# Graph-convolution kernel on one core: Euler pieces in the pauses of the tridiagonalization, and a re-ordered Newton step

## The reference, cut to what matters

```python
h = relu(layernorm(x)); x = x + L0(h)        # Euler stage
h = relu(layernorm(x)); x = x + L1(h)        # graph convolution in the eigenbasis
h = relu(layernorm(x)); x = x + L2(h)
h = relu(layernorm(x)); x = x + L3(h)
# L0: 8 steps on h = x @ fc_w.T + fc_b, with w_eff = w * clip(d, 0, 1) @ w.T
f = sigmoid(alpha)[:, None] * 0.5 * (adj @ h - h) + h @ w_eff - h + x0
h = h + f / 8
# L1: deg = row sums + column sums - diagonal of A
L_norm = deg**-0.5 * (diag(deg) - A) * deg**-0.5
_, U = eigh(L_norm)
out = U @ (relu((U.T @ h) @ W1 + b1) @ W2 + b2)
```

## Time and profile before

| | us |
|---|---|
| median of 3 runs | 4941.13 (4937.12 to 4941.86) |
| the profiled execution, its own time | 4943.4 |
| its span | 4941.6 |
| PE (matmul) busy | 3781.6 (77%) |
| DVE busy | 3279.5 (66%) |
| ACT busy | 1064.3 (22%) |
| POOL busy | 413.0 (8%) |

### The profile page before, as it was taken

The page is one execution under the profiler, slowest core; times in us unless marked ns, Lnnn a source line. Parts: engine busy times, 40 slices in busy tenths (PEclk is TensorE's granted clock), DMA queues, the critical chain, the costliest instruction groups (busy, mean ns, idle before and its releaser), DMA issues.

```text
span 4941.6 us, 71519 instructions
## 1 busy us (share of the span) xinstructions
PE 3781.6 (77%) x20546; PEld 1897.0 (38%) x20546; DVE 3279.5 (66%) x20976; ACT 1064.3 (22%) x4173; POOL 413.0 (8%) x1793
## 2 busy tenths in 40 slices
PE   4777777777778888888875667748965957599998
PEld 2333333333333333333354333425542623244433
DVE  5777777878888888888877898998822122202323
ACT  1111111222222222222201111101112122314542
POOL 0000000000000000000022221101100000000000
PEclk8999999999999999999956878879977978689998
DMA  2000000000000000000000000000000000000000
GB/s 86 2 1 1 2 1 1 2 1 1 2 1 1 1 2 1 1 1 1 1 1 1 1 1 1 1 0 1 1 0 0 0 17 0 0 0 0 0 0 34
DMA packets 3109, 21.11 MB, mean 4 GB/s; under 512 B 432, under 2 KB 560, under 8 KB 1072
## 3 DMA queue, kind: packets, MB, share of 16 engines
q1 hardware_dynamic: 2736, 16.85, 0.9%
HBM read 12.66 MB, written 4.19 MB: 3 GB/s over the span
## 4 chain that ended last, share of the span: by engine, by line
PE 48%; DVE 44%; ACT 3%; issue 3%; DMA 0%; POOL 0%; DVEq 0%; SPq 0%; POOLq 0%; ACTq 0%
PE ps L554 7%; PE ps L524 7%; PE ps L834 6%; DVE jq L1245 4%; PE ps L558 3%; PE ps L546 3%; DVE C L1424 2%; PE ps L841 2%; DVE tsc L1408 2%; DVE WG L1365 2%; DVE tsc L1418 2%; PE ps L530 2%; DVE tsc L1398 2%; DVE TMP L1360 2%; PE ps L806 1%
## 5 line engine op out<-in xcount | busy, mean ns | idle before, releaser
L546 PE MATMUL ps<-eye,same 128*128 128x512 f32 x2040 | 1200.4, 672 | 0.0
L563 PE MATMUL ps<-dots,ones 128*128 128x3 f32 x1020 | 199.2, 265 | 368.1 <-DVE dots L1245 367.5
L563 PEld LDWEIGHTS ps<-dots,ones 128*128 128x128 f32 x1020 | 161.4, 197 | 805.2 <-DVE dots L1245 803.8
L554 PEld LDWEIGHTS ps<-C 128*32 128x32 f32 x10200 | 255.2, 114 | 522.3 <-DVE C L1424 441.0
L554 PE MATMUL ps<-C 128*32 128x131 f32 (+39 forms) x10200 | 373.8, 277 | 76.1 <-DVE C L1424 21.3
L1079 ACT ACTIVATE sz<-C,tsc 128x4 f32<-128x4 f32 (+3 forms) x510 | 151.6, 297 | 1022.6 <-DVE tsc L1415 1022.6
L546 PEld LDWEIGHTS ps<-eye,same 128*128 128x128 f32 x2040 | 328.9, 203 | 0.0
L524 PE MATMUL ps<-C,LT 128*128 128x512 f32 x512 | 244.2, 622 | 91.9 <-ACT C L1071 91.9
L834 PE MATMUL ps<-C,V 128*128 128x512 f32 (+1 forms) x504 | 287.5, 727 | 8.5 <-issue 7.5
L884 POOL TENSOR_TENSOR xm<-C,WK 128x4 f32<-128x4 f32 (+3 forms) x510 | 101.0, 198 | 2275.0 <-DVE C L1424 1917.2
L1077 ACT ACTIVATE tsc<-tsc 128x1 f32<-128x1 f32 x510 | 103.4, 203 | 841.4 <-DVE tsc L1378 841.4
(11 more groups left out here) (468 smaller groups left out, 7127.4 us busy)
## 6 DMA issues: line engine op xcount, KB each, us to landing
out_x<-X SPq DMA_DIRECT2D x4, 1024.0 KB, 3.9
X<-in_x SPq DMA_DIRECT2D x2, 1280.0 KB, 20.5
X<-in_x SPq DMA_DIRECT2D x1, 1536.0 KB, 16.8
eye<-in_eye SPq DMA_DIRECT2D x1, 1026.0 KB, 9.4
WK<-in_adj SPq DMA_DIRECT2D x1, 1024.0 KB, 4.9
adjT<-in_adjT SPq DMA_DIRECT2D x1, 1024.0 KB, 7.0
WK<-in_below SPq DMA_DIRECT2D x1, 1024.0 KB, 11.2
V<-in_wih SPq DMA_DIRECT2D x1, 1024.0 KB, 4.9
```

What stands on the lines that cost most here:

```text
L546: mm(ps[:, 7, 0:n], ident, eye[:, 0, 0:n], start=True, stop=True)
L554: mm(ps[q * QUAD:(q + 1) * QUAD, 0, 0:c + n], SI[:, b, 0, 2 * j:2 * j + 1].broadcast_to([P, QUAD]), AS[:, b, q, k * QUAD:P + n], start=(b ...
L563: mm(ps[:, 3, 0:3], ones[:], dots[:], start=True, stop=True).then_inc(S["dots_ps"], 1)
```

## The change

1. The Euler work leaves the front and the tree. `plan_gaps` cuts it into pieces and puts each into one of the two pauses of a reflection (`pause`); a pause without a piece keeps its idle matmul. A piece whose data come from an eviction may only stand in a first pause after the reflection in which ScalarE evicts (`at`); the pieces of a unit follow each other pause by pause. ScalarE evicts at most one item per reflection, after `saved`; POOL adds to X after its unit vector.
2. `ln_root(0)` stands directly behind `table_fill` on ScalarE.
3. The idle matmul goes to bank 2; the panel's transposes to banks 2 and 3, since Euler uses 4 to 7.
4. In a Newton step the coefficients are formed in place in QF, with the factor -4 in c, one paired product, and the absolute value on ScalarE; X8 is formed before the clamp.
5. At the start of a level POOL scales LE by -4 gap and makes L8; VectorE does neither.
6. Below level 7 the two products for F2 are one instruction.

```diff
+REFLECTIONS = N - 2
...
+    def __init__(self):
+        self.tensor, self.scalar, self.pool = {}, {r: [] for r in range(REFLECTIONS + 2)}, {r: [] for r in range(REFLECTIONS + 2)}
+        self.gap, self.seen = 0, {}
+    def at(self, key, r):
+        while len(self.scalar[r]) > 0:
+            r += 1
+        self.scalar[r].append(key)
+        self.seen[key] = r
+        return r
+    def unit(self, key, parts):
+        for part, needs in enumerate(parts):
+            g = max([self.gap] + [2 * self.seen[n] for n in needs])
+            self.tensor[g] = key + (part,)
+            self.gap = g + 1
+        return self.at(key, g // 2 + 1 if g % 2 == 0 else g // 2 + 2)
+def plan_gaps():
+    p = Gaps()
+    p.at(("fill", 0), 0)
+    last = ("fill", 0)
+    for u in range(EULER):
+        p.unit(("table", u), [[last]] * ((u + 1) // 3 + 1))
+        last = ("table", u)
+    p.unit(("out", 0), [[last]] * 4)
+    last = ("out", 0)
+    for u in range(EULER + 1):
+        p.unit(("w", u), [[last]] * KB)
+        last = ("w", u)
+    first = 1
+    for t in range(4 * TILES):
+        g, k, j = tile_of(t)
+        free = [("tile", t - 4)] if t >= 4 else [last]
+        if k is None:
+            if j == 0:
+                for h in range(8):
+                    first = p.at(("input", 8 * g + h), first) + 1
+            p.unit(("tile", t), [free + [("input", 8 * g + 2 * j + 1)]] * 2)
+        elif k == EULER:
+            p.unit(("tile", t), [free + [("tile", t - 1 - j)]])
+        else:
+            r = p.unit(("tile", t), [free] + [[("tile", t - j - 4 + mb)] for mb in range(KB)] + ([[]] if k == 0 else []))
+            if k == 0:
+                p.pool[r + 1].append(t)
+                first = r + 1
+    return p
...
+                o = ps[:, 4 + u % 2, nb * D:(nb + 1) * D]
+                if u > 0:
+                    for mb in range(KB):
+                        mm(o, LT[:, mb, nb * P:(nb + 1) * P], w_of[(u - 1) % 2][:, mb, :], start=(mb == 0), stop=False)
+                m = mm(o, ones[0:1, :], r_row(k) if u > 0 else rows[0:1, 0, :], start=(u == 0), stop=True)
+                if nb == KB - 1:
+                    m.then_inc(S["w_tile_ps"], 1)
+            def tile_part(t, part):
...
+                        pe.wait_ge(S["w_tile_sb"], EULER + 1)
+                if k is None:
+                    pe.wait_ge(S["x0_ready"], 8 * g + 2 * j + 2)
+                    for nb in range(2 * part, 2 * part + 2):
+                        m = turn(ps[:, bank, nb * P:(nb + 1) * P], B0[:, j, nb, :])
+                    if part == 1:
+                        m.then_inc(S["eu_ps"], 1)
+                    return
+                last = {EULER: 0, 0: 1 + KB}.get(k, KB)
+                if part == 0:
+                    if k == EULER:
+                        pe.wait_ge(S["eu_sb"], t - j)
+                    for q in range(4):
+                        m = mm(ps[:, bank, q * D:(q + 1) * D], x0T[:, q, j * P:(j + 1) * P],
+                               W["fcT"] if k == EULER else G[:, k, :], start=(q == 0), stop=(part == last and q == 3), skip_group_check=True)
+                elif part <= KB:
+                    mb = part - 1
+                    pe.wait_ge(S["eu_sb"], t - j - 4 + mb + 1)
+                    m = mm(ps[:, bank, :], LT[:, mb, j * P:(j + 1) * P], state(k + 1)[:, :, mb, :],
+                           start=False, stop=(part == last), skip_group_check=True)
                 else:
+                    m = mm(ps[:, bank, :], ident, w_of[EULER % 2][:, j, :].unsqueeze(1).broadcast_to([P, 4, D]),
+                           start=False, stop=True, skip_group_check=True)
+                if part == last:
                     m.then_inc(S["eu_ps"], 1)
...
+            def pause(r, h):
+                piece = PLAN.tensor.get(2 * (r - 1) + h)
+                if piece is None:
+                    keep_clock(HEAT[r // P][h])
                     return
...
+                kind, i, part = piece
+                if kind == "table":
+                    table_part(i, part)
+                elif kind == "out":
+                    out_part(part)
+                elif kind == "w":
+                    w_part(i, part)
+                else:
+                    tile_part(i, part)
...
+                pause(r, 0)
...
+                pause(r, 1)
...
+                        g, _, i = tile_of(t_)
+                        pool.wait_ge(S["eu_sb"], t_ + 1)
+                        xb = X[:, 4 * g:4 * g + 4, i, :]
+                        g_.tensor_tensor(xb, xb, B1[:, :, i, :], ALU.add).then_inc(S["x_added"], 1)
...
+                        g_.tensor_tensor(grid(LEf, lv), grid(LEf, lv), col_grid(cn["gap4"], lv), ALU.mult).then_inc(S["le_ready"], 1)
+                        product(L8[:, 0:4], cn["t1"], cn["hg"])
+                        product(L8[:, 4:8], L8[:, 0:4], cn["hg"], ALU.add)
+                        scaled(L8[:, 4:8], L8[:, 4:8], -1.0, ALU.mult)
...
             table_fill()
-            for u in range(EULER):
-                table_evict(u)
-            table_out()
...
+                for kind, i in PLAN.scalar[r]:
+                    if kind == "table":
+                        table_evict(i)
+                    elif kind == "out":
+                        table_out()
+                    elif kind == "w":
+                        w_evict(i)
+                    elif kind == "input":
+                        euler_input(i)
+                    else:
+                        euler_evict(i)
...
+                    act.wait_ge(S["a_ready"], lv * NEWTON + it + 1)
+                    fn(small("absa"), QF[:, 1, :], ACT.Abs).then_inc(S["abs_ready"], 1)
...
-                    for u in EULER_SLOTS[lv * NEWTON + it]:
-                        euler_unit(u)
...
-                step(tt(L8[:, 0:4], cn["t1"], cn["hg"], ALU.mult))
-                step(stt(L8[:, 4:8], L8[:, 0:4], -1.0, cn["hg"], ALU.mult, ALU.subtract))
-                step(stt(MU[0], gap, 0.25, L8[:, 0:4], ALU.mult, ALU.add))
-                step(tt(grid(LEf, lv), grid(LEf, lv), col_grid(gap, lv), ALU.mult))
+                step(ts_(cn["gap4"], gap, -4.0, None, ALU.mult))
+                step(stt(MU[0], cn["t1"], 0.5, cn["hg"], ALU.add, ALU.mult))
...
+                        if it == 0:
+                            dve.wait_ge(S["le_ready"], lv + 1)
                         for jb in range(KB):
                             go(ttr(TTf[:, big[jb]], TTf[:, big[jb]], LEf[:, big[jb]], fsum[:, 8 + jb:9 + jb]))
                         ch.wait()
                     dve.wait_ge(S["pq_ready"], i + 1)
-                    if it > 0 or lv > 0:
...
-                    stt(QF, twice(fsum[:, 0:4], 4), 1.0, Q6[:, 0:4, :], ALU.add, ALU.mult).then_inc(S["qf_ready"], 1)
+                    step(stt(QF, twice(fsum[:, 0:4], 4), 1.0, Q6[:, 0:4, :], ALU.add, ALU.mult))
                     step(tt(pair(UU), twice(fpf), Q6[:, 3:5, :], ALU.mult))
-                    dve.wait_ge(S["qf_ready"], 2 * i + 1)
-                    AC = MK
-                    step(tt(pair(CM), QF[:, 1:3, :], pair(UU), ALU.subtract))
-                    step(tt(CM[:, 4:8], CM[:, 4:8], fsum[:, 8:12], ALU.add))
-                    a, c, b = CM[:, 0:4], CM[:, 4:8], QF[:, 3, :]
-                    step(tt(PR[:, 0:4], a, a, ALU.mult))
-                    step(tt(PR[:, 4:8], c, b, ALU.mult))
-                    step(stt(cn["disc"], PR[:, 4:8], -4.0, PR[:, 0:4], ALU.mult, ALU.add))
+                    step(ts_(pair(X8), QF[:, 0:3:2, :], 0.0, None, ALU.is_gt))
...
+                    dve.wait_ge(S["a_ready"], i + 1)
+                    a = QF[:, 1, :]
+                    step(stt(QF[:, 2, :], QF[:, 2, :], -4.0, fsum[:, 8:12], ALU.mult, ALU.add))
+                    step(tt(pair(PR), QF[:, 1:3, :], QF[:, 1:4:2, :], ALU.mult))
+                    step(tt(cn["disc"], PR[:, 0:4], PR[:, 4:8], ALU.add))
                     ts_(cn["disc"], cn["disc"], 1e-34, None, ALU.max).then_inc(S["disc_ready"], 1)
-                    step(ts_(ND[:, 0:4], c, -4.0, None, ALU.mult))
-                    v.tensor_copy(ND[:, 4:8], b).then_inc(S["qf_ready"], 1)
-                    step(ts_(pair(X8), QF[:, 0:3:2, :], 0.0, None, ALU.is_gt))
                     dve.wait_ge(S["pm_ready"], i + 1)
                     v.copy_predicated(L8, X8.bitcast(U32), PM8).then_inc(S["lo_ready"], 1)
-                    step(stt(cn["t2"], a, -1.0, a, ALU.mult, ALU.max))
                     step(stt(pair(MK), twice(a), 0.0, pair(zeros_ones), ALU.is_gt, ALU.subtract))
                     dve.wait_ge(S["sqrt_ready"], lv * (NEWTON + 1) + it + 1)
-                    step(tt(cn["t1"], cn["t2"], cn["root"], ALU.add))
-                    dve.wait_ge(S["qf_ready"], 2 * i + 2)
-                    put(pair(ND), pair(MK), twice(cn["t1"]))
-                    step(v.reciprocal(cn["rden"], ND[:, 0:4]))
-                    step(tt(cn["t1"], ND[:, 4:8], cn["rden"], ALU.mult))
+                    dve.wait_ge(S["abs_ready"], i + 1)
```

(65 more changed lines are left out.)

123 lines of the change are left out of this document (39 added, 84 removed).

## The result

Median 4861.05 us (4845.71 to 4867.59, four runs) against 4939.12 us before (4934.58 to 4941.86): ratio 0.9833, 95% interval 0.9808 to 0.9858; the medians are 78 us apart. Forecast: 4875.5.

The account below looks back on a forecast made before the run. VectorE's serial chain bounds the kernel; in reflections TensorE executes its links, in the tree VectorE waits for ScalarE. Gains 123.6 less losses 58 give 65.6 us; 4943.4 becomes 4877.8, 2.3 less against the median: 4875.5 us, range 4850 to 4902.

Parts of the forecast that it names:

- Front: Before the reflections: Euler tables no longer delay the square root VectorE waits for; 18.3 us gained.
- Tree, waits: Tree of merges: VectorE no longer waits for ScalarE's roots behind Euler evictions; 63.0 us gained.
- Tree, port: Tree: small VectorE operations no longer held up behind POOL's additions into X; 4.3 us gained.
- Newton step and set-up: Tree: shorter VectorE chain in 72 steps, 36 us gained; set-up of a level, net 2 us gained.
- w pieces: Reflections: 18 w pieces in second pauses overrun by 0.23 us each; 4 us lost (0 to 11).
- Clock in the w stretch: Reflections with w pieces: TensorE's clock, once cold, warms late; twelve cold reflections, 24 us lost.
- Transposes: Reflections: pieces of two transposes let the clock fall, three cold reflections in each of four groups; 24 us lost.
- X additions: Reflections: 16 POOL additions beside VectorE, free if inside its wait for TensorE, at most 21 us; 2 us taken.
- w and transposes stay cold throughout: Rival for the reflections: losses 140 us instead of 58, 4957 us at the bound; chance 0.15.
- The clock does not notice: Rival for the reflections: the clock stays as before, losses only 8 us, 4825 us; chance 0.12.
- Euler tiles can't hold it: Rival, reflections 49 to 424: tile pieces lose the clock, 5045 us with 85 more cold reflections; chance 0.08.
- Abs: Rival in the Newton steps: Abs evicts ScalarE's square root table, some 2 us per step, 5015 us; chance 0.03.

Follow-up runs that it names:

- euler_alone: The kernel after with the Newton step and level set-up of before; 4884.4 us (0.9893).
- turn_idle: The kernel after with an idle matmul of 256 columns behind each of the 32 pieces of two transposes; 4840.8 us (0.9791).
- x_one: The kernel after with each of POOL's 16 additions into X cut to one element per partition; 4839.8 us (0.9793).
- x_quarters: The kernel after with each of POOL's 16 additions into X cut in four, one per reflection; 4837.8 us (0.9801).
- experiment 2: The kernel after with POOL's additions into X cut to one element per partition (4839.8 us) or in four (4837.8 us).
- newton_alone: The kernel before with only the new Newton step and level set-up, Euler staying in the tree; 4918.2 us (0.9955).

## Why the prediction was right, and where not

The time lay 14 us under the forecast and inside its own range, and the direction and the gains came as worked out; but two terms of the losses were wrong by 20 us, in opposite directions, so that the number came so near is in part luck.

- **Front**: 18.3 forecast, 18.2 measured.
- **Tree, waits**: 63.0 forecast. By groups, VectorE's idle time before those two lines fell by 38.8 and 24.0 us in `euler_alone`, and before L1661 by another 2.7.
- **Tree, port**: mis-sized. I read it off one four-element line, 4.3 us. In `euler_alone` all VectorE lines of the tree together are 11.1 us shorter than before; wide two-input lines had been held up too. Waits and port sum to 76.6, and the tree's length says 75.1.
- **Newton step and set-up**: 36 + 2 forecast, 34.1 measured with ScalarE free. The step's working stands almost to the number (1.41 and 0.50 us where 1.40 and 0.43 were forecast, so 0.42 us won per step instead of 0.50); POOL's late operations are the 4.5 us at L1699 and 3.0 at L1684 in the first levels. What the sum did not say is that the term needs the other one: with Euler still in the tree it is worth 17.5.
- **w pieces**: 4 us forecast for the overrun, 0.21 us each, so right; the one-row matmul, taken at 0.40, takes 0.42 from its start to the next instruction. **Clock in the w stretch**: the step that failed, 24 us. It said that w would stay cold once cold, because the same matmuls ran at 0.51 in the tree. In the reflections they stand among L610, L614 and L619, and were granted 0.97 over four of them, two in second pauses (206 to 217 us):

```profile
206.00:217.00 11.00, 9.81 (x113) 7.40 (x111) 8.31 (x75) 2.68 (x17) 0.66 (x4) 0.97 0.01 2
```

Over reflections 18 to 43 the clock was 0.89, before the change 0.94. Reflections 18 to 44 cost 7.3 us in all, 3.8 of them the overruns: the clock's part is 3 to 4 us. A clock read off the same instructions in another stage doesn't carry over. Why the w units of the tree ran cold stays open: in the kernel before TensorE was busy for 21.31 of these 22 us and granted 0.50 throughout:

```profile
2532.00:2554.00 22.00, 21.31 (x80) 17.88 (x79) 11.39 (x72) 0.90 (x3) 2.94 (x15) 0.50 0.00 0
```

- **Transposes**: 24 forecast, 20 measured by `turn_idle`. The number was right, its reason not shown: the Trainium skill, TensorE: Matmul & The Clock Gate, section "Part 4: PE-mode transpose", says that they don't count for the clock, and no run here tells that apart from their being short.
- **X additions**: the other step that failed. "Nothing if they land while VectorE waits for L554" (now L610), and 2 us taken between 0 and 21. They do land there, but in front of L1473, which is then held until 1.26 us later, longer than the wait. By `x_one` and `x_quarters` they cost 21 to 23 us, the upper bound; about 16 of them stand at the additions themselves, and the rest is spread or, as the profiles of experiment 2 suggest, a clock that falls behind them.
- **Rivals**: none came true. *w and transposes stay cold throughout* fails for both: w ran at 0.89, and the transposes cost what the forecast, not the rival, gave them. *The clock does not notice* is refuted by 0.92 against 0.94 and by the groups of transposes; *Euler tiles can't hold it* by LT and four-matmul pieces that cost 0.00 us; Abs brought no table load; no piece waited for its data in a second pause.
- **Signs**: the front, the tree's length, L1749 and the missing table loads came as said. The 0.94 became 0.92, but reflections 15 to 44 were not cold for long, and the stage grew by 31.6 us in the profiled run, by 51 only in a median one, where 50 to 60 were forecast.

The losses that I forecast as 58 us are about 51 in a median run: additions 21 to 23, transposes 20, w and tables 11. That is 7 us less, and the gains of 123.6 came to 129.3 (4 in the tree, and 2 in the rest, for which I had no term and which is spread: that stage lies between 1349 and 1357 us in the profiles): together the 13 to 14 us by which the time lay under the forecast. The two large errors, 20 us each, cancel by luck.

## What to carry to other kernels

Work that replaces idle matmuls is free if it is as long as they were; set every shape of it against the pause and pad the short ones (256 idle columns behind 32 short pieces gave 20 us). Place what POOL does beside a serial VectorE chain by what VectorE runs at that moment, and cut it to fit the chain's idle time: the same 16 additions cost some 20 us whole and nothing measurable in quarters. When two gains share an engine, measure one with the other present.

## What the runs showed of the hardware

- A VectorE instruction of three elements per partition and two inputs took 1.30 us instead of 0.22 beside POOL's addition of 128x512, and 0.24 beside one of 128x128 (0.45 us) that had started 0.23 us earlier. Beside one of that size that started 0.03 us later it took 0.50.
- Plain matmuls with the identity over 2 x 128 columns (0.69 us) let the clock fall between panel updates as two transposes (0.41 us) did; the granted clock over 880 to 900 us was 0.83 and 0.68, against 1.00 with 256 idle columns behind the transposes.
- TensorE was busy 21.31 of 22 us with the w units of the tree and granted 0.50 throughout; with the same matmuls in the reflections it was granted 0.97 over 11 us.
- The kernel before spreads over 22 us in the ten runs beside `newton_alone`, after over 22 in its four. The profiles show the clock falling in different reflections of one and the same code.
- With w in first pauses alone and all other pieces nine reflections later, the median is 14 us higher and TensorE spends 96 us more at 0.50 away from the panel updates.
